# Decoder layer on eight cores: three filler matmul units per attention step in place of four, and the normalizer's small DMAs issued by SyncE in place of GpSimd

## The chip, the cores and the metric

The kernel runs on one Trainium2 chip, on all 8 of its cores. Each core computes half of the query rows of one of four sequences; the cores do not talk to each other. The metric is the device time in microseconds of the slowest core.

## The reference

One transformer layer with the normalization behind each residual, in float32, x of shape (4, 4096, 1024), 16 heads of 64, hidden size 3072:

```python
def reference(x, Wq, Wk, Wv, Wo, w_gate, w_up, w_down):
    x = _layernorm(x + attn(x, Wq, Wk, Wv, Wo))   # causal softmax attention, scale 1/8
    x = _layernorm(x + ffn(x, w_gate, w_up, w_down))
    return x

def ffn(x, w_gate, w_up, w_down):                 # int weights, times 1/127
    h = silu(x @ wg.T) * (x @ wu.T)
    return h @ wd.T
```

## The kernel before

All activations are kept feature-major (features on partitions, tokens along the free axis). A core holds the whole sequence's keys and values (T = 4096) and 2048 of its queries, taken as every second block of 128 tokens, so that the causal work is even. The text cuts the program into three parts: attention (to about 1283 us), the output projection with the first normalization, and the feed-forward part with the second. The change touches the first part alone.

Attention runs in NPASS = 4 passes, numbered 0 to 3, of four heads each. A pass `p` needs keys, values and queries of its heads. Pass 0's are projected ahead of everything (`proj_gen(0)`, run to its end); those of pass `p + 1` are projected during pass `p`, as filler between the attention matmuls. Between two passes stands `c_compute` (lines 278 to 325), a serial chain that finds the bound by which the exponent is shifted.

`attention_pass` (lines 388 to 490) loops over 2 head pairs (`hp`) and 4 banks of 512 queries (`bank`); bank number b sees 8b + 8 key blocks (`kb`), so the banks have 8, 16, 24 and 32 steps and a pass has 2 x 80 = 160 steps. One step:

- `emit_s` of the next key block: two score matmuls into `sp` (lines 398 and 403, one head each, on the two halves of TensorE's rows), then one exponential over both heads on ScalarE (line 415), 128 x 1024 elements. `sp` and `pt` have two buffers each. In the last 8 steps of a bank the block lies on the causal diagonal: the tile narrows to 384, 256 and 128 queries, and VectorE multiplies two masks (lines 421 and 424).
- `fill(rate)`: takes `rate` units from the filler generator (line 471).
- `emit_pv` of the current block: two matmuls of the probabilities with the values into `op` (line 443).

At a bank's end VectorE copies both heads' outputs and row sums out of PSUM (lines 477 and 483, four copies), and the first `emit_pv` of the next bank waits for the last of them. SyncE stores the row sums in DRAM (`ldram`, line 486).

The filler. `proj_gen(p + 1)` has 448 units, one matmul each. For each of 8 slices of 512 tokens there are 16 key units of 512 columns (line 226) and then 32 value units of 256 columns (line 240); after these come 4 query slices of 16 units of 512 columns (line 264). The text calls the 192 key and query units wide and the 256 value units narrow. Eight units make a group that VectorE then copies out of PSUM (`pp`, two buffers). The slices of x come through GpSimd's DMA queue with a cast to bf16 into `xstg`, two buffers: each load waits until the slice before the last is used up (lines 219 and 257). The weights of a pass come at the generator's start on the same queue (lines 194 to 196), with no wait of their own.

Behind the 448 units the filler chain has `norm_gen(p - 1)`, 10 more units, in passes 1, 2 and 3 (in pass 3 it is the only filler); for the last pass it runs by itself at the end (line 508). It turns the row sums of pass `p - 1` into reciprocals and scales the outputs. When it is called, ahead of the pass, its first part (lines 330 to 334) is emitted: the queue waits for the row sums' stores and loads them into `lrecA`. Its first unit is a reciprocal on VectorE, and a store `linvd<-lrecB` that waits for it; its second is eight loads `lpair<-linvd` that wait for that store (`s_lwb`); each of the other eight is one float32 matmul that spreads `lpair` over the partitions (line 366, shown as two instructions) and a multiplication on VectorE (line 371). Before the change all of these DMAs stand on GpSimd's queue, between the loads of x and the weights. Each queue issues in program order, and an instruction that waits holds everything behind it.

The semaphores that matter: `s_ldm` (row sum stores landed), `s_lpr` (`lrecA` landed), `s_nrm` (reciprocal done), `s_lwb` (`linvd` landed), `s_lp` (`lpair` landed), `s_xst` (x landed), `s_evV` (VectorE copies).

Of the kernel before, what the change touches and what calls it, by code (L numbers as in the profile page):

```python
# [42 lines left out]
def build_program(cfg):  # L43
# [16 lines left out]
    nc = bass.Bass("TRN2", target_bir_lowering=False, num_devices=1)  # L60
# [22 lines left out]
    with st:  # L83
# [15 lines left out]
        s_evV = Sem(st, nc, "s_evV")  # L99
# [5 lines left out]
        s_ldm = [Sem(st, nc, f"s_ldm{i}") for i in range(4)]  # L105
        s_lpr = Sem(st, nc, "s_lpr")
        s_lwb = Sem(st, nc, "s_lwb")
        s_lp = [Sem(st, nc, f"s_lp{i}") for i in range(8)]
        s_cb = Sem(st, nc, "s_cb")
        s_nrm = Sem(st, nc, "s_nrm")  # L110
# [217 lines left out]

        def norm_gen(p):
            for i in range(4):  # L330
                nc.gpsimd.wait_ge(s_ldm[i].h, s_ldm[i].n)
            s_lpr.inc(nc.gpsimd.dma_start(
                lrecA[:, :], ldram[4 * p:4 * p + 4].rearrange("h (a f) -> (h a) f", f=LRF)), 16)
            lrd = s_lpr.n

            def gen():
                nc.vector.wait_ge(s_lpr.h, lrd)
                s_nrm.inc(nc.vector.reciprocal(lrecB[:, :], lrecA[:, :]))
                nc.gpsimd.wait_ge(s_nrm.h, s_nrm.n)
                s_lwb.inc(nc.gpsimd.dma_start(  # L340
                    linvd[4 * p:4 * p + 4].rearrange("h (a f) -> (h a) f", f=LRF),
                    lrecB[:, :]), 16)
                wb = s_lwb.n
                yield
                idxs = [(2 * p + g, s) for g in range(2) for s in range(NQS)]
                ldone = {}
                def issue(i):
                    gcx, s = idxs[i]
                    j = lp_slot[0]
                    lp_slot[0] = (j + 1) % 8  # L350
                    nc.gpsimd.wait_ge(s_lwb.h, wb)
                    nc.gpsimd.wait_ge(s_evV.h, ldone.get(("f", j), 0))
                    s_lp[j].inc(nc.gpsimd.dma_start(
                        lpair[j][:, :],
                        linvd[2 * gcx:2 * gcx + 2, s * 512:s * 512 + 512]), 16)
                    ldone[i] = (j, s_lp[j].n)
                for i in range(len(idxs)):
                    issue(i)
                yield
                for i, (gcx, s) in enumerate(idxs):  # L360
                    j, lv = ldone[i]
                    pi = gidx[0] % 2
                    gidx[0] += 1
                    nc.tensor.wait_ge(s_evV.h, pp_free[pi])
                    nc.tensor.wait_ge(s_lp[j].h, lv)
                    s_prj.inc(nc.tensor.matmul(pp[pi][:, :], emat[:, :], lpair[j][:, :],
                                               start=True, stop=True))
                    tgt = s_prj.n
                    nc.vector.wait_ge(s_prj.h, tgt)
                    q0 = s * 512  # L370
                    s_evV.inc(nc.vector.tensor_mul(
                        ofm[:, gcx * TOWN + q0: gcx * TOWN + q0 + 512],
                        ofm[:, gcx * TOWN + q0: gcx * TOWN + q0 + 512], pp[pi][:, :]))
                    pp_free[pi] = s_evV.n
                    ldone[("f", j)] = s_evV.n
                    yield
            return gen()

        def chaing(*gens):
            for g in gens:  # L380
                yield from g
# [113 lines left out]
        for p in range(NPASS):  # L495
            parts = []
            if p + 1 < NPASS:
                parts.append(proj_gen(p + 1))
            if p >= 1:
                parts.append(norm_gen(p - 1))  # L500
            filler = chaing(*parts) if parts else None
            filler = attention_pass(p, filler, rate=4)
            if filler is not None:
                for _ in filler:
                    pass
            if p + 1 < NPASS:
                c_compute(p + 1)
        for _ in norm_gen(NPASS - 1):
            pass
# [184 lines left out]
        for idx, (ncx, s) in enumerate(wo_iters):  # L694
            q0 = s * 512
            i = idx % 2
            j = idx % 4
# [101 lines left out]
        for fs in range(NFS):  # L799
# [79 lines left out]
            for dc in range(NCH):  # L879
# [11 lines left out]
                for nh in range(NH2):  # L891
                    c0 = nh * 512
                    i = 0
# [110 lines left out]
```

## Time and profile before

| what | us |
|---|---|
| median of 2 runs | 2122.15 (2077.97 and 2166.32) |
| profiled execution | 2078.7 |
| its span on the slowest core (core 4) | 2077.7 |
| spans of the eight cores | 2051.9 to 2077.7 |
| TensorE busy | 1618.6 (78%) |
| ScalarE busy | 824.3 (40%) |
| VectorE busy | 613.9 (30%) |
| GpSimd busy | 183.8 (9%) |
| mean granted TensorE clock of the cores | 0.861 to 0.873 |

Busy times are unions over the whole span, which has stages with different limits, so their shares say nothing of a single stage. The rows of the trace all come from core 4. The clock column of a view is the clock that TensorE was granted, as a share of its full speed: 1.00 is the upper of its two levels (2.4 GHz), 0.50 the lower (1.2 GHz), and what lies between is a mean over a stretch that had both.

### The profile page before, as it was taken

Reading aid. Unit: us, or ns where it says so; the run is one execution under the profiler, and the core shown is the slowest. Engines: PE = TensorE matmul, PEld = TensorE weight load, DVE = VectorE, ACT = ScalarE, POOL = GpSimd, SP = SyncE. Lnnn points to the kernel's source line nnn. Section 1 sums busy time; section 2 is a strip of 40 time slices with the busy share of each in tenths; the row PEclk is TensorE's granted clock in tenths of the full one; section 3 lists DMA queues with packets and bytes.
Section 4 is the critical chain, followed back from the end, with each engine's and each line's share of the span. In section 5 each row is a group of like instructions: output and inputs, shape, how many; then the busy total and the mean of one; then the engine's idle time right before and its main releaser. Section 6 shows DMA issues by size and latency. Waiting matters only on the chain. (4 is left out here: it accounts for less than half of the span.)

```text
span 2077.7 us, 22780 instructions; the slowest of 8 cores (2051.9 to 2077.7 us)
## 1 busy us (share of the span) xinstructions
PE 1618.6 (78%) x7240; PEld 625.2 (30%) x7240; DVE 613.9 (30%) x1436; ACT 824.3 (40%) x999; POOL 183.8 (9%) x221
## 2 busy tenths in 40 slices
PE   3858998679977689887577674877998879998862
PEld 1423443124432134321111111323443334443320
DVE  1234332253332432421521212454211111111224
ACT  0015665756654767537367670331111011112022
POOL 1010000010000000010100001001221112221000
PEclk9887999879997799978578785988999999999985
DMA  7692333063340433320000003325777657777522
GB/s 100 94 136 36 62 62 61 1 93 62 51 72 2 57 56 62 61 43 1 3 1 1 1 1 58 91 65 52 69 74 71 61 51 71 71 72 71 86 56 81
DMA packets 224112, 115.31 MB, mean 55 GB/s; under 512 B 152030, under 2 KB 215520, under 8 KB 224000
## 3 DMA queue, kind: packets, MB, share of 16 engines
q0 software_dynamic: 215104, 96.94, 38.1%
q1 hardware_dynamic: 8896, 16.91, 2.6%
q8 instruction: 65, 1.06, 0.2%
q14 instruction: 47, 0.39, 0.1%
HBM read 201.66 MB, written 8.65 MB: 101 GB/s over the span
## 5 line engine op out<-in xcount | busy, mean ns | idle before, releaser
L415 ACT ACTIVATE pt<-sp,cbias 128x1024 bf16<-128x1024 f32 (+3 forms) x640 | 619.7, 984 | 384.2 <-PE sp L403 380.3
L443 PE MATMUL op<-pt,vbuf 128*65 128x512 bf16 (+3 forms) x1280 | 376.4, 379 | 144.5 <-DVE pt L424 57.4
L398 PE MATMUL sp<-qbuf,kbuf 64*128 64x512 bf16 (+3 forms) x640 | 239.2, 383 | 2.1 <-DVE cbias L324 2.1
L403 PE MATMUL sp<-qbuf,kbuf 64*128 64x512 bf16 (+3 forms) x640 | 239.5, 383 | 0.0
L443 PEld LDWEIGHTS op<-pt,vbuf 128*65 128x65 bf16 x1280 | 118.8, 117 | 291.2 <-issue 259.8
L899 PE MATMUL dps<-hbuf,wdd 128*128 128x512 bf16 x768 | 179.8, 393 | 34.1 <-DVE y L910 32.9
L841 PE MATMUL gps<-x1b,wgb 128*128 128x512 bf16 x768 | 186.9, 387 | 24.0 <-DVE x1b L809 13.0
L850 PE MATMUL ups<-x1b,wub 128*128 128x512 bf16 x768 | 184.7, 384 | 6.8 <-DVE hbuf L862 6.8
L858 ACT ACTIVATE sgb<-gps 128x512 bf16<-128x512 f32 x96 | 57.3, 597 | 304.5 <-PE gps L841 295.1
L226 PE MATMUL pp<-xstg,wkb 128*128 128x512 bf16 x512 | 142.7, 414 | 40.4 <-DMA xstg<-xfm 40.4
L240 PE MATMUL pp<-wvb,xstg 128*128 128x256 bf16 x1024 | 150.1, 278 | 0.6
L862 DVE TENSOR_TENSOR hbuf<-sgb,ups 128x512 bf16<-128x512 bf16 x96 | 66.1, 688 | 285.2 <-PE ups L850 285.2
L421 DVE TENSOR_TENSOR pt<-pt,mka 128x128 bf16<-128x128 bf16 x128 | 28.8, 225 | 366.9 <-ACT pt L415 366.7
L398 PEld LDWEIGHTS sp<-qbuf,kbuf 64*128 64x128 bf16 x640 | 58.1, 94 | 250.4 <-issue 248.5
L574 ACT ACTIVATE ysq<-y 128x512 bf16<-128x512 f32 x64 | 40.0, 625 | 219.7 <-DVE y L910 134.8
L899 PEld LDWEIGHTS dps<-hbuf,wdd 128*128 128x128 bf16 x768 | 75.0, 100 | 140.9 <-issue 62.8
L841 PEld LDWEIGHTS gps<-x1b,wgb 128*128 128x128 bf16 x768 | 74.4, 99 | 124.3 <-issue 42.8
L850 PEld LDWEIGHTS ups<-x1b,wub 128*128 128x128 bf16 x768 | 76.0, 99 | 100.7 <-issue 12.8
L297 ACT ACTIVATE qsq<-kbuf 128x512 bf16<-128x512 bf16 x64 | 39.4, 627 | 165.1 <-DVE qbuf L272 142.6
L240 PEld LDWEIGHTS pp<-wvb,xstg 128*128 128x128 bf16 x1024 | 85.0, 99 | 48.8 <-issue 34.9
L264 PE MATMUL pp<-xstg,wqb 128*128 128x512 bf16 x256 | 72.6, 421 | 27.6 <-DMA xstg<-xq 27.4
L252 DVE CAST vbuf<-pp 128x256 bf16<-128x256 f32 x128 | 54.4, 425 | 120.0 <-PE pp L240 118.6
(83 smaller groups left out, 1218.2 us busy)
## 6 DMA issues: line engine op xcount, KB each, us to landing
xstg<-xfm POOLq DMA_DIRECT2D x32, 1024.0 KB, 9.4
xstg<-xq POOLq DMA_DIRECT2D x16, 1024.0 KB, 9.3
wgb<-wgT POOLq DMA_DIRECT2D x48, 256.0 KB, 4.3
wub<-wuT POOLq DMA_DIRECT2D x48, 256.0 KB, 5.4
wdd<-wdT POOLq DMA_DIRECT2D x16, 768.0 KB, 8.1
xres<-xq SPq DMA_DIRECT2D x32, 256.0 KB, 3.3
yout<-y SPq DMA_DIRECT2D x4, 2048.0 KB, 6.9
wqb<-wqT POOLq DMA_DIRECT2D x4, 512.0 KB, 8.0
```

The lines of the kernel that those rows point to most:

```text
L226: return nc.tensor.matmul(ps[:, 0:512], wkb[pb][:, m * PD + nk * 128: m * PD + nk * 128 + 128], xs[:, m * 512:(m + 1) * 512], start=(m == ...
L240: return nc.tensor.matmul(ps[:, 0:PD], xs[:, m * 512 + jb * 128: m * 512 + jb * 128 + 128], wvb[pb][:, m * PD:(m + 1) * PD], start=(m == 0 ...
L264: return nc.tensor.matmul(ps[:, 0:512], wqb[pb][:, m * PD + nq * 128: m * PD + nq * 128 + 128], xs[:, m * 512:(m + 1) * 512], start=(m == ...
L398: nc.tensor.matmul(sp[buf][:, js * 128: 512], kbuf[pb][0:64, hp * T + kb * 128: hp * T + kb * 128 + 128], qbuf[pb][0:64, hp * TOWN + qbase ...
L403: s_s.inc(nc.tensor.matmul(sp[buf][:, 512 + js * 128: 1024], kbuf[pb][64:128, hp * T + kb * 128: hp * T + kb * 128 + 128], qbuf[pb][64:128 ...
L415: s_exp.inc(nc.scalar.activation(pview, sview, AF.Exp, bias=cbias[pb][:, 0:1]))
L443: lastpv = nc.tensor.matmul(ops[hl][:, js * 128: 512], vbuf[pb][:, kb * VGW + (2 * hp + hl) * 65: kb * VGW + (2 * hp + hl) * 65 + 65], pt[ ...
L841: lastg = nc.tensor.matmul(gps[:, :], wgb[wi][:, m * 128:(m + 1) * 128], x1b[:, m * FFS + c0: m * FFS + c0 + 512], start=(m == 0), stop=(m ...
L850: last = nc.tensor.matmul(ups[:, :], wub[wi][:, m * 128:(m + 1) * 128], x1b[:, m * FFS + c0: m * FFS + c0 + 512], start=(m == 0), stop=(m ...
L858: s_fact.inc(nc.scalar.activation(sgb[:, :], gps[:, :], AF.Silu))
L862: s_fdve.inc(nc.vector.tensor_mul(hbuf[:, hc * FFS + c0: hc * FFS + c0 + 512], sgb[:, :], ups[:, :]))
L899: last = nc.tensor.matmul(dps[i][:, :], wdd[wi2][:, hc * 128: hc * 128 + 128], hbuf[:, hc * FFS + c0: hc * FFS + c0 + 512], start=(hc == 0 ...
```

## The change

Two edits in the attention part. `norm_gen` issues its DMAs, and makes its waits, on SyncE's queue instead of GpSimd's. `attention_pass` is called with `rate=3` instead of `rate=4`: `fill` takes three units per step.

```diff
         def norm_gen(p):
             for i in range(4):
-                nc.gpsimd.wait_ge(s_ldm[i].h, s_ldm[i].n)
-            s_lpr.inc(nc.gpsimd.dma_start(
+                nc.sync.wait_ge(s_ldm[i].h, s_ldm[i].n)
+            s_lpr.inc(nc.sync.dma_start(
                 lrecA[:, :], ldram[4 * p:4 * p + 4].rearrange("h (a f) -> (h a) f", f=LRF)), 16)
             lrd = s_lpr.n
 
             def gen():
                 nc.vector.wait_ge(s_lpr.h, lrd)
                 s_nrm.inc(nc.vector.reciprocal(lrecB[:, :], lrecA[:, :]))
-                nc.gpsimd.wait_ge(s_nrm.h, s_nrm.n)
-                s_lwb.inc(nc.gpsimd.dma_start(
+                nc.sync.wait_ge(s_nrm.h, s_nrm.n)
+                s_lwb.inc(nc.sync.dma_start(
                     linvd[4 * p:4 * p + 4].rearrange("h (a f) -> (h a) f", f=LRF),
                     lrecB[:, :]), 16)
@@
-                    nc.gpsimd.wait_ge(s_lwb.h, wb)
-                    nc.gpsimd.wait_ge(s_evV.h, ldone.get(("f", j), 0))
-                    s_lp[j].inc(nc.gpsimd.dma_start(
+                    nc.sync.wait_ge(s_lwb.h, wb)
+                    nc.sync.wait_ge(s_evV.h, ldone.get(("f", j), 0))
+                    s_lp[j].inc(nc.sync.dma_start(
                         lpair[j][:, :],
                         linvd[2 * gcx:2 * gcx + 2, s * 512:s * 512 + 512]), 16)
@@
-            filler = attention_pass(p, filler, rate=4)
+            filler = attention_pass(p, filler, rate=3)
```

TensorE, in pass 1, where the filler runs out: the last query units and the first matmuls of the normalizer (`pp<-lpair,emat`), and the first step that has no filler. Before:

```order
L264 MATMUL pp1<-xstg1,wqb0 128x512 x4
L443 MATMUL op0<-pt1,vbuf1 65x512
L443 MATMUL op1<-pt1,vbuf1 65x512
L398 MATMUL sp1<-qbuf1,kbuf1 128x512
L403 MATMUL sp1<-qbuf1,kbuf1 128x512
L366 MATMUL pp0<-lpair0,emat 128x512
L366 MATMUL pp1<-lpair1,emat 128x512
L443 MATMUL op0<-pt0,vbuf1 65x512
L443 MATMUL op1<-pt0,vbuf1 65x512
```

And now, the same place in the filler:

```order
L264 MATMUL pp1<-xstg1,wqb0 128x512 x3
L443 MATMUL op0<-pt0,vbuf1 65x512
L443 MATMUL op1<-pt0,vbuf1 65x512
L398 MATMUL sp0<-qbuf1,kbuf1 128x512
L403 MATMUL sp0<-qbuf1,kbuf1 128x512
L264 MATMUL pp1<-xstg1,wqb0 128x512
L443 MATMUL op0<-pt1,vbuf1 65x512
L443 MATMUL op1<-pt1,vbuf1 65x512
L398 MATMUL sp1<-qbuf1,kbuf1 128x512
L403 MATMUL sp1<-qbuf1,kbuf1 128x512
L366 MATMUL pp0<-lpair0,emat 128x512
```

The number of matmuls is the same. Before, 448 units at 4 a step end with step 112 of the pass, inside the last bank but one; now, at 3 a step, with the first unit of step 150, ten steps before the end. In both, one pair of `op` matmuls and one pair of `sp` matmuls stand between the last projection unit and the first matmul that reads `lpair`.

GpSimd's queue from the last x load of pass 0 on (`xstg<-xq` are the query slices), as a difference:

```order
 L186 DMA xstg<-xfm 128x8x512 x8
 L186 DMA xstg<-xq 128x8x512 x4
-L332 DMA lrecA<-ldram 32x256
 L191 DMA wqb<-wqT 128x8x256
 L191 DMA wkb<-wkT 128x8x256
```

With `lrecA` gone from this queue, nothing stands between the last x load of one pass and the weights of the next: they and the next two x slices are no longer held until the row sums of the pass are stored.

SyncE's queue in passes 0 and 1 (after it, the same for the others):

```order
-L486 DMA ldram<-lstg 1x512 x64
+L486 DMA ldram<-lstg 1x512 x16
+L332 DMA lrecA<-ldram 32x256
+L486 DMA ldram<-lstg 1x512 x14
+L340 DMA linvd<-lrecB 32x256
+L353 DMA lpair<-linvd 2x512 x8
+L486 DMA ldram<-lstg 1x512 x2
```

The normalizer's DMAs now stand between the row sum stores of the seventh and of the last bank of the pass.

## Rows read from the trace of the kernel before

**Rows 1.** Windows, passes 0 to 3: us; busy PE, PEld, DVE, ACT, POOL; PEclk, DMA share, GB/s.
```profile
170.40:411.50 241.10, 207.33 (x1088) 81.60 (x1088) 70.59 (x212) 156.07 (x162) 8.73 (x10) 0.93 0.28 45
438.30:704.80 266.50, 225.45 (x1106) 87.07 (x1106) 80.45 (x227) 158.43 (x164) 13.47 (x19) 0.89 0.27 42
728.90:991.40 262.50, 223.26 (x1106) 86.19 (x1106) 80.29 (x227) 157.53 (x164) 13.45 (x19) 0.90 0.27 43
1015.50:1258.00 242.50, 170.27 (x656) 45.20 (x656) 52.03 (x170) 152.95 (x160) 4.68 (x9) 0.76 0.00 1
```

**Rows 2.** Timeline, pass 0: start, us, engine, line; a wide-filled step, then a narrow-filled one.
```profile
250.78 0.39 PE L398 MATMUL sp<-qbuf,kbuf 64*128 64x512 bf16 x1
...
251.10 1.04 PE L226 MATMUL pp<-xstg,wkb 128*128 128x512 bf16 x4
...
251.97 0.59 PE L443 MATMUL op<-pt,vbuf 128*65 128x512 bf16 x2
...
252.50 0.39 PE L398 MATMUL sp<-qbuf,kbuf 64*128 64x512 bf16 x1
...
253.80 0.39 PE L398 MATMUL sp<-qbuf,kbuf 64*128 64x512 bf16 x1
```

**Rows 3.** Timeline, pass 0: steps without filler, two exponentials a row.
```profile
380.76 2.13 ACT L415 ACTIVATE pt<-sp,cbias 128x1024 bf16<-128x1024 f32 x2 [0.20 <-PE sp L403]
...
383.09 2.13 ACT L415 ACTIVATE pt<-sp,cbias 128x1024 bf16<-128x1024 f32 x2 [0.20 <-PE sp L403]
```

**Rows 4.** Windows: pass 0's filled banks 2 and 3, query units, empty bank; pass 3's banks 2, 3.
```profile
208.80:243.90 35.10, 33.29 (x196) 14.49 (x192) 11.49 (x33) 24.05 (x24) 1.79 (x3) 1.00 0.39 61
243.90:290.60 46.70, 44.97 (x260) 19.82 (x256) 13.70 (x37) 32.95 (x32) 2.56 (x3) 1.00 0.44 69
303.20:335.30 32.10, 26.28 (x132) 10.80 (x128) 9.80 (x29) 15.14 (x16) 1.75 (x2) 0.84 0.52 82
371.10:411.50 40.40, 29.60 (x128) 7.69 (x124) 5.49 (x20) 32.81 (x34) 0.00 (x0) 0.88 0.00 1
1071.80:1104.00 32.20, 23.36 (x98) 5.99 (x96) 5.66 (x21) 23.38 (x24) 0.00 (x0) 0.82 0.00 1
1104.00:1145.60 41.60, 31.33 (x130) 8.03 (x128) 5.62 (x21) 31.97 (x32) 0.00 (x0) 0.83 0.00 1
```

**Rows 5.** Timeline, TensorE: a change of bank at full clock; a filled step at half clock.
```profile
246.81 0.59 PE L443 MATMUL op<-pt,vbuf 128*65 128x512 bf16 x2 [1.58 <-DVE lstg L483]
...
438.94 0.63 PE L398 MATMUL sp<-qbuf,kbuf 64*128 64x512 bf16 x1
...
442.20 0.50 PE L398 MATMUL sp<-qbuf,kbuf 64*128 64x384 bf16 x1
```

**Rows 6.** Who waited for whom in pass 1 (438 to 704): total us, times, longest.
```profile
PE pp L366 <- DMA lpair<-linvd: 6.6, 1, 6.6
...
PE pp L264 <- DMA xstg<-xq: 3.0, 1, 3.0
```

**Rows 7.** The normalizer in pass 1: its timeline, and the window that holds it.
```profile
622.50 0.54 POOL L340 DMA_DIRECT2D linvd<-lrecB  x1 [18.96 <-DVE lrecB L338]
624.88 4.30 POOL L353 DMA_DIRECT2D lpair<-linvd  x8 [1.85 <-DMA linvd<-lrecB]
626.78 3.75 PE L366 MATMUL pp<-lpair,emat 2*128 2x512 f32 x4 [6.57 <-DMA lpair<-linvd]
...
618.10:647.40 29.30, 22.73 (x43) 6.59 (x42) 7.84 (x10) 5.57 (x5) 4.73 (x9) 0.59 0.01 2
```

**Rows 8.** DMA issues of the whole run: median us to landing.
```profile
xstg<-xq POOLq DMA_DIRECT2D x16, 1024.0 KB, 9.3
```

**Rows 9.** Tile `lrecA`, all four passes; its loads' time to landing.
```profile
DMA to landing us min/median/max: 1.9/2.6/3.4
```

**Rows 10.** Timeline, the end of attention: last row sum stores, first load of the normalizer.
```profile
1255.73 1.64 SPq L486 DMA_DIRECT2D ldram<-lstg  x2
...
1258.78 0.53 POOL L332 DMA_DIRECT2D lrecA<-ldram  x1 [230.38 <-DMA ldram<-lstg]
```

## The prediction

> **What bounds the kernel now.** I read the windows of the four passes first. Passes 0, 1 and 2 take 241.1, 266.5 and 262.5 us, pass 3, which has no projection in it, 242.5 [rows 1]: 448 filler matmuls cost a pass next to nothing, so a filled pass must have slack in its empty part. The timeline shows where. A full-width step with four wide units takes 1.72 us, from 250.78 to 252.50, and TensorE never stops: scores 0.32, filler 0.87, `op` pair 0.53. With four narrow units it takes 1.30, to 253.80 [rows 2]. Two steps without filler take 2.33 us, one 1.165, and there the exponential sets the pace, two in 2.13 us and 0.20 of waiting [rows 3]; TensorE's own work is 0.32 + 0.53 = 0.85, so it idles 0.31 in each. Before the change a pass has 112 filled steps and 48 empty ones: TensorE-bound first, ScalarE-bound after.
>
> The clock adds to it. The filled banks 2 and 3 ran at a granted clock of 1.00, the bank with the query units at 0.84, the empty bank at 0.88, and pass 3's at 0.82 and 0.83 [rows 4]. The falls to half clock come after TensorE waited or had little to do. At half clock a wide-filled step takes 3.26 us, 438.94 to 442.20 [rows 5].
>
> **The rate.** The same 448 units now need 149 1/3 steps, and 10 2/3 stay empty. A wide unit takes 0.87 / 4 = 0.22 us, a narrow one half, 0.11. A step with three wide units then takes 1.72 - 0.22 = 1.50, with three narrow ones 1.19, still just above 1.165. At full clock and with every step of full width:
> - before: 48 wide steps x 1.72 + 64 narrow x 1.30 + 48 empty x 1.165 = 221.7 us
> - after: 64 x 1.50 + 85.3 x 1.19 + 10.7 x 1.165 = 209.9 us, 11.8 less.
>
> Not all of this arrives. At a change of bank TensorE idles 1.58 us behind VectorE's fourth copy though it has four wide units there [rows 5]; six changes, three steps each, lose a unit and gain nothing: 18 x 0.15 = 2.7 back. In the narrow masked steps the chain exponential, mask, `op` is about as long as the filled step; some 14 of them give back about 2.7. That leaves 6.4. The same step-by-step sum makes the filled banks of before 35.0 and 47.0 us; measured are 35.1 and 46.7 [rows 4]. For after it gives them 31.9 and 42.7, and pass 3's empty ones, which are a floor, took 32.2 and 41.6 with the clock at 0.82: the filler becomes nearly free.
>
> Two smaller terms per pass. A slice of query units was used up in 4 x 1.72 = 6.9 us while its successor takes 9.3 to land [rows 8], and TensorE waited 3.0 us in pass 1 [rows 6]. A slice now lasts 5 1/3 x 1.50 = 8.0; two slices cover 2.2 us more, I take 2.0. And the clock: the step sum at full clock gives pass 0 of before 227 us; measured are 241.1, of which some 4 is the waiting for x and 10 the half clock, most of it in the query bank and the empty steps. Those steps now have filler and shorter waits; I take 4 of the 10 back, the fall at the start of a pass stays. Bounds: 0 and 8.
>
> So 6.4 + 2.0 + 4 = 12.4 us per pass, three passes, -37. What is late next in each step is again TensorE, but with ScalarE 0.03 us behind it in the narrow ones. Pass 3 has only the ten normalizer units; three instead of four a step moves one matmul by a step: 0.
>
> **The normalizer on SyncE.** In the timeline its chain is 622.50 (store), 624.88 (first load), 626.78 (first matmul); TensorE waits 6.57 us at it, and the stretch around it runs at a clock of 0.59 [rows 6, 7]. At rate 3 the same two pairs of matmuls stand between the last query unit and the first `lpair` matmul, so the wait stays. What is queued behind the waiting instructions on SyncE is only row sum stores: in passes 1 and 2 those of the last bank, issued after the normalizer is through, and four `lstg` buffers stand before VectorE would wait for one. Cost 0. GpSimd's issue took 2.38 us from store to load; SyncE's last row sum store, whose issue ended at 1255.73 + 1.64 = 1257.37, had landed by 1258.78 [rows 10], 1.4 later, for a smaller transfer. I take the hop as equal, bounds -1 and +1 us for each of four chains: 0, between -4 and +4.
>
> The Trainium skill, "DMA: Bandwidth & Descriptors", section "Latency and other measured facts", puts the first byte at about 0.6 us for a DMA issued from SyncE and about 1 us from GpSimd. By it three hops in four chains would save 3 x 4 x 0.4 = 4.8 us and the sum would be five lower; no row here times the same transfer on both queues.
>
> The new thing is what GpSimd now does early. With `lrecA` off its queue, the three weight loads for the next projection follow the last x load at once and two x slices follow as their buffers come free, in passes 0 and 1. Their old place was under `c_compute`, where the filler did not wait for them, so issuing them earlier gains 0. But in pass 1 they are in flight when the normalizer's store and loads run. The row for a small load beside such traffic: `lrecA` took up to 3.4 us to land, 1.9 at the least [rows 9], 1.5 more. Two transfers in the chain, once: +3; bounds 0 and +10, if each waits out half of a 9.3 us slice. The last x load of passes 0 and 1 shares with the weights too and its successor has none to wait for; under 1 us each, within the rounding.
>
> Sum: -37 + 3 = -34. The profiled execution took 2078.7 us around a span of 2077.7, close to the lower of the two runs shown (2077.97); the median 2122.15 is only the mean of it with 2166.32. My forecast stands against 2078.7: 2078.7 - 34 = about 2045 us, 1.6% less. Two per cent is about what a measurement of this kernel can tell from no change.
>
> **Rivals.**
> - Only the step sum arrives: the half clock keeps its 10 us a pass and the wait for x its 3. 3 x 6.4 = 19, less 3 for the normalizer: 2063 us. For it: the falls also come at masked steps, which stay light. Against: the filled banks 2 and 3 had none [rows 4].
> - More arrives: the clock stays up in the whole filled stretch, 8 us a pass, and the wait for x goes: 3 x 17 = 51, 2028 us. The floor is pass 3: 242.5 less the 20 us of its own normalizer leaves 222, so three passes cannot give more than about 58, 2020 us.
> - The normalizer is caught behind the early loads: +10 in place of +3, 2052 us.
> - Slower: thinner filler lets the clock fall at every change of bank. Four narrow units a step kept it at 1.00 there, none did not (pass 3, 0.82 and 0.83) [rows 4], and three lie between. Where it falls with filler present TensorE is the bound: a narrow step goes from 1.19 to about 2.4 us, and over a fall of three such steps that is 3.5 us. Seven changes in three passes are 21 x 3.5 = 74 us: 2045 + 74 = 2119 us. It decides from about ten falls on, 34 / 3.5; below that the change still gains. Against it: three narrow units still leave TensorE busy all through an ordinary step (1.19 of 1.19), and a full-width step with no filler at all held full clock in pass 0.
> - The edits change nothing that counts, since filler moves only from where TensorE is the bound to where it has slack, and ScalarE takes the gain back by waiting more often at the masked steps: 2078 us. Against it: 15 us of idle TensorE in 48 steps are real.
>
> On the slower rival, the Trainium skill, "TensorE: Matmul & The Clock Gate", section "Part 1: The HAM clock gate (the "warmup" mystery)", says that "the default state is throttled, and activity releases the throttle". The rows on the clock above agree in direction: 0.88 and 0.82 where TensorE is thinly loaded, 1.00 where it is full. By the rule alone thinner filler speaks for more falls in the filled part and fewer in what was empty.
>
> **How the numbers follow.** Forecast, 2035 to 2055: 0.52. Step sum only, near 2063: 0.17. More arrives, near 2028: 0.15. Normalizer caught: 0.06. Nothing: 0.05. Slower by the clock: 0.05. The unknown costs (clock 0 to 8 a pass, hops -4 to +4, collision 0 to +10) carry the forecast to 2022 and 2070, and that range leaves out mainly the last two cases. Faster by over 2% means under 2037: the "more" case and the lower edge of the forecast, 0.20. Slower by over 2%, over 2120, is the upper part of the clock rival: 0.04. Within 2%: 0.76.
>
> **What would show it.** In the profile of the changed kernel: wide steps of 1.50 and narrow ones of 1.19 us; full banks 2 and 3 near 32 and 43 us; query units ending inside the last bank of a pass; the three filled passes near 229, 257 and 251 us and pass 3 unchanged; TensorE's wait for `xstg<-xq` under 2 us a pass; its wait for `lpair` at 6 to 7 us in pass 2 and longer in pass 1; weight loads issued before the pass ends. I am wrong if the clock in banks 1 to 3 falls well below 1.00, if narrow steps stay at 1.30, or if the wait at `lpair` grows past 15 us.

## The result, and the profile after

The changed kernel took 2068.68 us (median of 21 executions) where the kernel before took 2088.11 (median of 18). The ratio is 0.9906, with a 95% interval from 0.9874 to 0.9937: about 20 us less, a real gain, but one inside the 2 per cent and well short of the 34 us forecast. The profiled execution took 2055.78 us around a span of 2054.7, 22.9 under that of before. That agrees with the ratio, and it is the number the forecast of 2045 stands against: 11 us too fast. In some executions one half of the chip ran at a lower clock and took some per cent longer; the medians are over all executions, the ratios leave those out.

First the windows of passes 0 to 3 on core 4, the columns as in [rows 1]:

```profile
164.90:404.00 239.10, 211.66 (x1090) 80.26 (x1090) 71.26 (x214) 158.31 (x164) 13.15 (x15) 0.92 0.41 60
429.60:694.00 264.40, 226.76 (x1106) 84.43 (x1106) 80.38 (x227) 159.00 (x164) 13.15 (x15) 0.87 0.37 55
717.90:974.00 256.10, 227.02 (x1106) 84.67 (x1105) 80.01 (x227) 158.97 (x164) 8.76 (x10) 0.89 0.27 42
998.20:1238.00 239.80, 168.23 (x656) 44.55 (x654) 51.96 (x169) 153.26 (x160) 0.00 (x0) 0.77 0.00 1
```

Against [rows 1] the passes are 2.0, 2.1, 6.4 and 2.7 us shorter; 12 had been forecast for each filled one. The clock column is what to look at: 0.93, 0.89, 0.90 before, 0.92, 0.87, 0.89 now. It did not rise, it fell. The early loads show in GpSimd's column of pass 0, 15 issues for 10 and 13.15 us for 8.73. In pass 1 it has 15 for 19, though the normalizer's nine are gone. The DMA share rose with them, from 0.28 to 0.41 and from 0.27 to 0.37.

One core is a thin basis for a few microseconds, so from here on I also use means over the eight cores of a profile, from the first score matmul of a pass to the start of its last, read in each core's timeline. "Half clock" is 2 x (1 - granted clock) x length, the time spent at the lower level. The last column ends with the issue of the first load of the output projection's weights.

| mean of 8 cores, us | pass 0 | pass 1 | pass 2 | pass 3 | last score to output projection |
|---|---|---|---|---|---|
| before | 238.5 | 260.9 | 259.9 | 234.7 | 30.7 |
| after | 232.6 | 258.9 | 250.1 | 233.8 | 28.3 |
| half clock before | 28.7 | 54.2 | 53.6 | 101.0 | |
| half clock after | 27.8 | 59.3 | 49.2 | 101.2 | |

Together 5.9 + 2.0 + 9.8 + 0.9 + 2.4 = 21 us, which is the ratio's 20. Pass 1 gained next to nothing, and the half clock kept its total.

The steps themselves are as the sum had them. TensorE's timeline on core 4, a step with three wide units (242.72 to 244.22) and one with three narrow ones (246.71 to 247.89):

```profile
242.72 0.39 PE L398 MATMUL sp<-qbuf,kbuf 64*128 64x512 bf16 x1
...
243.04 0.82 PE L226 MATMUL pp<-xstg,wkb 128*128 128x512 bf16 x3
...
244.22 0.39 PE L398 MATMUL sp<-qbuf,kbuf 64*128 64x512 bf16 x1
...
246.71 0.39 PE L398 MATMUL sp<-qbuf,kbuf 64*128 64x512 bf16 x1
...
247.03 0.50 PE L240 MATMUL pp<-wvb,xstg 128*128 128x256 bf16 x3
...
247.89 0.39 PE L398 MATMUL sp<-qbuf,kbuf 64*128 64x512 bf16 x1
```

Now the banks. The windows of pass 0's filled banks 2 and 3, of the fifth bank (the first of the second half) and of its last one, against [rows 4]:

```profile
200.90:234.70 33.80, 30.52 (x170) 12.23 (x168) 9.59 (x30) 23.96 (x24) 1.09 (x2) 0.95 0.20 33
234.70:277.80 43.10, 40.38 (x228) 15.91 (x226) 11.52 (x33) 32.99 (x32) 1.82 (x3) 1.00 0.31 50
277.80:292.60 14.80, 12.27 (x59) 4.49 (x56) 7.10 (x24) 6.25 (x8) 0.59 (x1) 0.77 0.46 72
348.00:401.00 53.00, 43.92 (x188) 14.03 (x184) 10.78 (x26) 32.43 (x31) 6.76 (x8) 0.89 0.93 129
```

Bank 3 took 43.10 at full clock; 42.7 was the step sum. Bank 2 took 33.80 at 0.95 where 31.9 was the sum. The fifth bank ran at 0.77. TensorE's timeline at its start shows how that comes about (a score pair that reads `qbuf,kbuf` opens each step):

```profile
277.77 0.38 PE L398 MATMUL sp<-qbuf,kbuf 64*128 64x512 bf16 x1
...
278.08 0.82 PE L226 MATMUL pp<-xstg,wkb 128*128 128x512 bf16 x3
281.10 1.04 PE L443 MATMUL op<-pt,vbuf 128*65 128x512 bf16 x2 [2.20 <-DVE pt L424]
282.07 0.50 PE L398 MATMUL sp<-qbuf,kbuf 64*128 64x384 bf16 x1
...
284.75 0.50 PE L398 MATMUL sp<-qbuf,kbuf 64*128 64x384 bf16 x1
...
287.22 0.28 PE L398 MATMUL sp<-qbuf,kbuf 64*128 64x256 bf16 x1
```

Three wide units end, TensorE idles 2.20 us behind VectorE's mask, and the `op` pair after it takes 1.04 in place of 0.59: the lower level. The next two steps, masked ones of 384 queries, take 2.68 and 2.47 us (from 282.07 and from 284.75); the one behind them takes 1.29. By 287 the clock is back.

Last the wait for the normalizer in pass 1. These are the waits of TensorE there on core 4; in [rows 6] they were 6.6 and 3.0 (as means of the eight cores `lpair` takes 12.2 now and 6.6 before):

```profile
PE pp L366 <- DMA lpair<-linvd: 9.6, 1, 9.6
PE pp L264 <- DMA xstg<-xq: 4.8, 1, 4.8
```

And the timeline around it, against [rows 7]:

```profile
630.30 0.88 POOL L186 DMA_DIRECT2D xstg<-xq  x1 [7.23 <-PE pp L264]
631.17 0.88 POOL L191 DMA_DIRECT2D wqb<-wqT  x1
...
645.19 0.88 POOL L186 DMA_DIRECT2D xstg<-xfm  x1 [11.38 <-PE pp L264]
653.46 0.88 POOL L186 DMA_DIRECT2D xstg<-xfm  x1 [7.38 <-PE pp L264]
655.44 0.31 SPq L340 DMA_DIRECT2D linvd<-lrecB  x1
661.87 2.84 SPq L353 DMA_DIRECT2D lpair<-linvd  x8
663.29 5.45 PE L366 MATMUL pp<-lpair,emat 2*128 2x512 f32 x6 [9.64 <-DMA lpair<-linvd]
```

The weight load goes out right behind the last `xstg<-xq` and two slices of the next projection follow, the second 2 us before the 32 KB store `linvd`. The store takes 655.44 to 661.87. The view of tile `linvd` gives its four landings:

```profile
DMA to landing us min/median/max: 1.4/1.4/6.3
```

Three take 1.4 us, the one beside the megabyte takes 6.3. The DMA issues of the run show the same of the larger loads: `xstg<-xq` has a median of 9.7 (9.3 in [rows 8]), and the weights, which now share with the last x load:

```profile
wqb<-wqT POOLq DMA_DIRECT2D x4, 512.0 KB, 13.4
```

### The profile page after: what moved, and what is told of

It reads as the page before. It is cut to its first block and busy times, and to the rows that moved or that the text cites. A ratio compares the mean times of both kernels' runs of the same rounds, so it can differ in the third digit from the quotient of the medians.

```text
span 2054.7 us, 22780 instructions; the slowest of 8 cores (2028.8 to 2054.7 us)
## 1 busy us (share of the span) xinstructions
PE 1621.6 (79%) x7240; PEld 617.6 (30%) x7240; DVE 612.3 (30%) x1436; ACT 828.1 (40%) x999; POOL 163.0 (8%) x181
## 5 line engine op out<-in xcount | busy, mean ns | idle before, releaser
L226 PE MATMUL pp<-xstg,wkb 128*128 128x512 bf16 x512 | 148.9, 409 | 40.3 <-DMA xstg<-xfm 39.6
L240 PE MATMUL pp<-wvb,xstg 128*128 128x256 bf16 x1024 | 164.0, 281 | 0.6
L421 DVE TENSOR_TENSOR pt<-pt,mka 128x128 bf16<-128x128 bf16 x128 | 28.8, 225 | 249.0 <-ACT pt L415 247.6
## 6 DMA issues: line engine op xcount, KB each, us to landing
wqb<-wqT POOLq DMA_DIRECT2D x4, 512.0 KB, 13.4
```

The costliest lines, as they stand in the source:

```text
L226: return nc.tensor.matmul(ps[:, 0:512], wkb[pb][:, m * PD + nk * 128: m * PD + nk * 128 + 128], xs[:, m * 512:(m + 1) * 512], start=(m == ...
L240: return nc.tensor.matmul(ps[:, 0:PD], xs[:, m * 512 + jb * 128: m * 512 + jb * 128 + 128], wvb[pb][:, m * PD:(m + 1) * PD], start=(m == 0 ...
```

## The experiments

All times are medians of 5 to 13 executions, each beside runs of the kernel before on the same chip; the interval of each ratio is the 95% one.

**The rate alone.** The kernel before, `norm_gen` left on GpSimd:

```diff
-            filler = attention_pass(p, filler, rate=4)
+            filler = attention_pass(p, filler, rate=3)
```

> The rate alone: three units a step, the normalizer's DMAs left on GpSimd's queue, so that the next pass's loads stay behind the row sums. Theory C (collision): the changed kernel lost time in passes 0 and 1 because the weights and x slices of the next projection, now issued early, slow the last x load and the normalizer's two small transfers. Then passes 0 and 1 are about 4 and 8 us shorter here than in the changed kernel (from first to last score matmul near 229 and 251 us, where the changed kernel has 232.6 and 258.9 as a mean over cores and before has 238.5 and 260.9), and the whole is about 10 us faster than the changed kernel: ratio to before 0.985. Theory K (clock): the gain was lost to falls of TensorE's clock at bank changes under thinner filler. Then passes 0 and 1 are as in the changed kernel and the ratio is 0.991 to 0.993 (the normalizer's hops on GpSimd cost 3 us more).

Measured: 0.9871 [0.9837, 0.9904], 2056.57 us. Filled passes 231.4, 253.3, 253.2: 7.1, 7.6 and 6.7 shorter than before. That is the step sum's 6.4 with 0.3 to 1.2 more. TensorE's wait for x falls from 4.0, 3.2 and 3.4 us to 2.4, 2.5 and 2.3 (means of the eight cores), 1.1 of the 2.0 on average. Of the 4 for the clock nothing came: the half clock is 27.2, 54.0 and 53.1 us.

**The queue alone.** The changed kernel with four units a step:

```diff
-            filler = attention_pass(p, filler, rate=3)
+            filler = attention_pass(p, filler, rate=4)
```

> The queue alone: the normalizer on SyncE, four units a step. Theory C: passes 0 and 1 get slower than before by the same collisions (3 to 10 us together), the four normalizer chains win about 1 us each; ratio 0.998 to 1.004, TensorE's wait for lpair in pass 1 over 10 us. Theory K: no collision of weight, ratio 0.998, wait for lpair in pass 1 near 5 us.

Measured: 1.0000 [0.9974, 1.0025]. Pass 1 takes 268.4, 7.5 longer than before; passes 0 and 2 are within 1.0. The wait for `lpair` in pass 1 is 10.8 on its slowest core. What the queue gives at the end of each chain (below) is paid back in pass 1.

**The early loads held back.** The changed kernel, with GpSimd waiting for the row sums again before it issues a new projection's loads, and all else on SyncE:

```diff
             parts = []
+            if p >= 1:
+                for i in range(4):
+                    nc.gpsimd.wait_ge(s_ldm[i].h, s_ldm[i].n)
```

> The changed kernel with one wait put back on GpSimd's queue: the loads of the next projection wait for the row sums of the pass, as before the change. Theory C: the best of all: pass 0 near 229, pass 1 near 250 us, pass 2 unchanged at 250; ratio 0.983 to 0.985. Theory K: as the changed kernel, 0.99.

Measured: 0.9848 [0.9820, 0.9876], 2054.90 us. Pass 1 takes 251.3, 7.6 less than with the change; pass 0 takes 230.6, 2.0 less; pass 2, where no early load was, 249.6 against 250.1. All four landings of `linvd` are short again, in the view of the tile:

```profile
DMA to landing us min/median/max: 1.4/1.4/1.5
```

and so is TensorE's wait in pass 1, by the list of waits:

```profile
PE pp L366 <- DMA lpair<-linvd: 4.8, 1, 4.8
```

**The same at four units a step**, which closes the square of rate and loads:

```diff
-            filler = attention_pass(p, filler, rate=3)
+            filler = attention_pass(p, filler, rate=4)
```

> The missing corner: normalizer on SyncE, loads held, four units a step. If the collision is all that cost the queue change its gain, pass 1 falls from 268.4 (queue alone) to about 259 us, the four chains keep their 2 us each, and the ratio is 0.995 to 0.998, where the queue alone gave 1.000. If instead the order of the loads does not matter at four units a step, 1.000 and 268 us.

Measured: 0.9955 [0.9921, 0.9988]. Pass 1 is 259.9 and not 268.4. Beside the kernel before, passes 1, 2 and 3 are 1.0, 2.1 and 2.3 us shorter and the end 2.4, 7.8 in all: that is SyncE's part. So the early loads cost 0.45% at rate 4 (to 1.0000) and 0.58% at rate 3 (0.9848 to 0.9906), 9 and 12 us of 2088. SyncE by itself gives 0.45% at rate 4 (from 1) and 0.23% at rate 3 (from 0.9871), 9 and 5 us. Each of these differences is about as large as the intervals it is made of, but passes and waits agree with all four.

**Three x buffers**, in the changed kernel, the loads early as there:

```diff
-        slot_free = [0, 0]
+        slot_free = [0, 0, 0]
...
-                slot = ts % 2
+                slot = ts % 3
...
-                slot = qs % 2
+                slot = (NKVS + qs) % 3
```

> The changed kernel with three buffers for the x slices, so that the last query slices are loaded a slice earlier. Both theories: TensorE's wait for xstg<-xq in passes 0 to 2 (3 to 4 us each) goes, and with it one fall of the clock each. If a wait costs only itself, 10 us less than the changed kernel (0.986); if the half clock after it costs as much again, up to 15. Theory C adds that the wait for lpair in pass 1 stays long (over 10 us), since the next projection's loads still run beside it.

Measured: 0.9704 [0.9675, 0.9732], 2026.64 us. The filled passes give 4.6, 2.5 and 2.3. The large part is ahead of them: pass 0 starts at 139.3 on the mean and not at 160.2. TensorE's waits in this stretch, first with the change (0 to 165), then here (0 to 140):

```profile
PE pp L226 <- DMA xstg<-xfm: 39.6, 5, 28.9
PE pp L264 <- DMA xstg<-xq: 16.0, 3, 8.4
```

```profile
PE pp L226 <- DMA xstg<-xfm: 28.5, 1, 28.5
PE pp L264 <- DMA xstg<-xq: 7.5, 2, 5.3
```

The first wait, for the first slice, stays; the others go or halve. The profile's stretches account for some 30 of the 42 us between the ratios 0.9906 and 0.9704; the profiled executions are 33.7 apart, and each ratio has an interval of about 6 us to either side. I did not place the rest. In pass 1 the last bank still holds the collision (pass 1 is 256.4, pass 2 247.8): TensorE waits 15.8 us for `lpair` there on the slowest core.

**Three buffers and the loads held**:

```diff
+            if p >= 1:
+                for i in range(4):
+                    nc.gpsimd.wait_ge(s_ldm[i].h, s_ldm[i].n)
```

> Held loads and three x buffers together. If collision and the wait for x add up: passes 0, 1, 2 near 226, 249, 247 us, the start of pass 0 some 22 us earlier than before the change (the x loads of the first projection), ratio 0.965. If three buffers make the collision harmless (loads early enough), no better than three buffers alone, 0.970.

Measured: 0.9699 [0.9673, 0.9725]. Pass 1 gives the 10 us (246.0), the ratio hardly any (0.9704 before): pass 2 is 1.6 longer and the rest is within the interval. With three buffers the ratio alone would not show the collision; the passes do.

**More filler at a change of bank.** The loads held, and six units in the first step of each bank:

```diff
-                        fill(rate)
+                        fill(6 if kb == 0 else rate)
```

> The version with the held loads, but six units instead of three in the first step of each bank, where TensorE otherwise idles behind VectorE's fourth copy. Theory K2: what ate the rest of the forecast are falls of TensorE's clock at the changes of bank, which four units a step did not have in the full banks (0 us at half clock in banks 2 and 3 of a pass before, 2 to 3 us each at three units). Then these falls become fewer, pass 0 goes from 230.6 to 226 to 228 us as a mean over cores, and the ratio from 0.985 to 0.980 to 0.982. Rival (units only): where a unit stands makes no difference; the filler only ends some eight steps earlier, pass 0 stays within 1 us of 230.6 and the ratio at 0.985.

Measured: 0.9769 [0.9734, 0.9805], 2039.79 us, 0.8% under the run with the loads held alone. Half clock of pass 0 falls from 25.6 to 13.3 us and the pass from 230.6 to 224.3. The windows of bank 3 and of the fifth bank, of this kernel (its slowest core, 2) and then of the run with the loads held (core 4):

```profile
239.20:281.60 42.40, 40.30 (x227) 16.22 (x227) 11.80 (x34) 32.96 (x32) 1.75 (x2) 1.00 0.37 57
281.60:293.00 11.40, 9.20 (x63) 3.98 (x59) 6.88 (x24) 6.24 (x8) 0.00 (x0) 1.00 0.35 58
```

```profile
238.40:283.00 44.60, 41.88 (x226) 16.19 (x226) 11.46 (x33) 32.99 (x32) 1.77 (x3) 0.96 0.30 48
283.00:297.80 14.80, 12.27 (x58) 4.46 (x56) 7.09 (x24) 6.24 (x8) 0.65 (x1) 0.77 0.46 72
```

The fifth bank goes from 14.80 at 0.77 to 11.40 at 1.00. The timeline of its first step shows the same wait, only shorter, and no fall: the `op` pair behind it has its 0.59:

```profile
281.96 1.04 PE L226 MATMUL pp<-xstg,wkb 128*128 128x512 bf16 x4
282.83 0.38 PE L240 MATMUL pp<-wvb,xstg 128*128 128x256 bf16 x2
284.95 0.59 PE L443 MATMUL op<-pt,vbuf 128*65 128x512 bf16 x2 [1.73 <-DVE pt L424]
```

This edit also moves units between steps, so in the sum of the pass the filler and the clock are mixed. The fifth bank of the changed kernel itself settles it: the same instructions were run there at three clocks. In order, core 1 in pass 2, core 1 in pass 1, core 4 in pass 2:

```profile
825.90:837.90 12.00, 9.52 (x60) 3.98 (x56) 7.11 (x24) 6.25 (x8) 0.66 (x1) 1.00 0.58 89
541.10:554.50 13.40, 10.92 (x58) 4.15 (x56) 7.01 (x24) 6.25 (x8) 0.63 (x1) 0.87 0.51 80
830.90:845.50 14.60, 12.11 (x58) 4.43 (x56) 6.97 (x24) 6.25 (x8) 0.58 (x1) 0.77 0.46 73
```

2 x (1 - 0.77) x 14.60 = 6.7 us of half clock cost 2.6 us of time, 0.4 for each.

The traces bear a count as well. Take as a fall any change of bank with over 1 us at the lower level in the 9 us behind the bank's first score matmul; there are 7 changes x 3 passes x 8 cores = 168. The kernel before has 77 falls, the changed one 119, the one with the loads held 111, and this one 60. Bank 2 is where this edit does not reach: it starts with narrow units, six of them are only 0.66 us of filler, and it falls in 22 of 24. But the sixth bank starts with six narrow ones too and has no fall, so the filler of the first step is not all that counts.

**The normalizer's store and loads early.** The loads held, and the normalizer's first two units (the reciprocal with its store, and the eight loads) put ahead of the projection:

```diff
+            ng = norm_gen(p - 1) if p >= 1 else None
+            if p >= 1:
+                parts.append(head(ng))
             if p + 1 < NPASS:
                 parts.append(proj_gen(p + 1))
             if p >= 1:
-                parts.append(norm_gen(p - 1))
+                parts.append(ng)
```

> The version with the held loads, with the normalizer's reciprocal and its nine small DMAs at the head of the filler instead of behind the 448 projection units; its matmuls stay at the end. If TensorE's wait for lpair is what starts the half-clock stretch at the normalizer (5 to 6 us of waiting, 30 us at half clock in the last bank of passes 1 and 2), both go: passes 1 and 2 shorter by 8 to 15 us each, ratio near 0.975. Rival: the normalizer's two-row float32 matmuls keep the clock down by themselves; then only the wait goes, 5 us a pass, ratio near 0.980, and the half clock stays above 20 us.

Measured: 0.9838 [0.9807, 0.9868] beside 0.9848: no difference in the ratio. Pass 1 takes 247.6 against 251.3 and pass 2 247.9 against 249.6. The wait is gone from the last bank of pass 1, which goes from 69.5 to 62.7 (the other banks give 3 us of that back), but 23.0 us of half clock stay in it (29.7 before). So the wait causes only the smaller part of the low clock around the normalizer.

**All of it, and the filler metered by columns.** Three buffers, loads held, normalizer early; each unit now yields its cost (wide 2, narrow 1, normalizer 2), and a step takes units until it has spent 4, or 10 at the start of a bank:

```diff
-                for _ in range(n):
-                    if next(filler, StopIteration) is StopIteration:
+                credit[0] += n
+                while credit[0] > 0:
+                    cost = next(filler, StopIteration)
+                    if cost is StopIteration:
...
+                    credit[0] -= cost or 2
...
-                        fill(rate)
+                        fill(10 if kb == 0 else rate)
```

> All of it, and the filler metered by columns: two wide or four narrow units a step (the same TensorE time), five or ten in a bank's first step. By the step rows a full step then takes 1.29 whatever its filler, in place of 1.51 and 1.19. Theory K2: with the load even and the change of bank filled, the clock falls less in the full banks and pass 0 ends near 218 to 223 us; ratio 0.945 to 0.955. Units only: about as three a step, pass 0 near 226, ratio near 0.957.

Measured: 0.9424 [0.9400, 0.9448], 1962.67 us, with the next one the fastest of all and 2.75% under three buffers with the loads held (0.9699). That is the gain of three edits together, the early normalizer, the filler at the change of bank and the metering; they were not taken apart at this point. A filled step gets about two wide or four narrow units, 0.44 us, where the change gives 0.66 in some and 0.33 in others. The last ten steps or so of a pass have no projection unit in either. None of the 168 changes of bank has a fall; TensorE's waits there are 1.27 to 1.74 us, where the changed kernel has 1.79 to 2.20 and 119 falls. Passes 0 and 1, pass 0's bank 3 and its fifth bank, and the last bank of pass 1, on the slowest core (6):

```profile
139.90:353.00 213.10, 197.46 (x1084) 77.47 (x1080) 69.51 (x209) 156.02 (x159) 7.86 (x9) 0.99 0.30 45
382.20:607.60 225.40, 211.69 (x1098) 81.25 (x1094) 76.88 (x219) 156.12 (x159) 7.87 (x9) 0.95 0.33 51
205.00:247.40 42.40, 40.79 (x229) 16.59 (x227) 11.54 (x34) 32.96 (x32) 1.75 (x2) 1.00 0.39 58
247.40:258.80 11.40, 9.51 (x68) 4.74 (x66) 7.09 (x25) 6.24 (x8) 0.00 (x0) 1.00 0.35 57
555.90:607.60 51.70, 48.64 (x183) 15.19 (x179) 14.81 (x33) 32.48 (x31) 0.11 (x1) 0.87 0.13 21
```

Pass 0 has 4.6 us of half clock left of 27.8, and takes 213.3 us. In passes 1 and 2 it is 24, and nearly all of that (19.8 in pass 1) in the last bank, where the normalizer stands. TensorE's timeline there shows where the level falls: the same four instructions go from 1.98 to 3.78 us after the second group, with no wait named ahead of them (13.7 us stay at the lower level on this core from 590.4 on):

```profile
585.53 1.98 PE L366 MATMUL pp<-lpair,emat 2*128 2x512 f32 x4
588.32 1.98 PE L366 MATMUL pp<-lpair,emat 2*128 2x512 f32 x4
591.60 3.78 PE L366 MATMUL pp<-lpair,emat 2*128 2x512 f32 x4
596.84 3.78 PE L366 MATMUL pp<-lpair,emat 2*128 2x512 f32 x4
```

**The normalizer's matmuls spread.** As above, with one normalizer unit behind each 48th projection unit and at a cost of 8:

```diff
+        def mixed(pg, ng):
+            for i, cost in enumerate(pg):
+                if ng is not None and i < 384 and i % 48 == 47:
+                    yield next(ng)
+                yield cost
```

> The column-metered version with one normalizer matmul behind every 48th projection unit instead of all eight behind the last. In the version before it the last bank of passes 1 and 2 took 53.6 us against pass 0's 40.1, with 20 us at half clock. If the normalizer's float32 matmuls are slow because they stand together at half clock (1.8 us each), alone among projections at full clock they take about half and passes 1 and 2 come to 218 to 221 us from 227; ratio 0.934 to 0.938. Rival: each costs the same wherever it stands, or pulls the clock down around it: 224 to 230 us, ratio 0.942 or above.

Measured: 0.9427 [0.9383, 0.9471], no change. But the profile differs: the half clock of pass 1 goes from 24.3 to 7.9 us and the pass from 226.5 to 221.1 (pass 2 from 227.0 to 221.8), while the stretches behind the two passes grow from 29.2 to 32.2 and 31.8. The edit itself does that: at a cost of 8 the filler costs 640 + 64 + 4 = 708 and a pass spends 160 x 4 + 8 x 6 = 688, so ten query units are left over and run behind passes 1 and 2. Spread singly, the two-row matmuls no longer bring the level down, but they are not free: the other seven banks of pass 1 are 6.9 us longer together, the last one 12.3 shorter. What is left of the gain, 2.4 and 2.6 us behind passes 1 and 2, is less than the ratio can tell.

## Why the prediction was wrong

**The step sum was right.** Wide steps of 1.51 and narrow ones of 1.19 us stand in the timeline (1.50 and 1.19 forecast); bank 3 took 43.1 for 42.7. The rate alone gave 7.1, 7.6 and 6.7 us a pass, for 6.4 by the steps and 12.4 in all.

**The step that failed is "I take 4 of the 10 back" with the wait's 2.0 beside it**, 6.0 of the 12.4 us a pass. The clock did come up where the prediction had it: in pass 0, the sixth bank, which had held the query units and the wait for x, went from 8.1 us of half clock to 1.3, and the last one, empty before, from 9.1 to 5.6. It fell elsewhere in exchange: bank 2 from 0 to 3.4, bank 3 from 0 to 1.3 and the fifth bank from 0 to 5.5 (means of the eight cores). In total 28.7 became 27.8.

And it moved to where it costs. In an empty step ScalarE is the bound, so a slow TensorE is mostly hidden: a full-width one takes 1.53 us at the lower level for 1.165, one with three narrow units 2.15 for 1.19. Bank by bank, over all cores and runs, each us of half clock goes with 0.40 to 0.47 us of time in the second to seventh of the eight banks of the filled passes (three units a step) and with 0.15 to 0.21 in the third to eighth of pass 3 (the slope over all cores of the runs). At 0.45 and 0.2, an estimate, the half clock of pass 0 cost about 10 us before, as the prediction had it, and about 12 after: not 4 back but 2 more.

The prediction held this as its slower rival, with 21 falls at 3.5 us. The mechanism was real; its size was not. A core has on average 15 falls at its 21 changes, but it had 10 before; each costs 1.5 us (3.4 us of half clock) to 2.6, and they offset a gain and no more. The experiment with more filler in the first step of each bank shows it by its other side: half the half clock gone, 6.3 us of pass 0, of which 12.3 x 0.4 is about 5. The argument "three narrow units still leave TensorE busy all through an ordinary step" looked at the ordinary step; the level is lost in the one that is not, at the change of bank, where the wait behind VectorE is longer the less filler stands before it (2.20 us behind three wide units, 1.73 behind six units).

The floor of 222 us that the prediction took from pass 3, by which three passes could give no more than 58 us, was none: pass 3 runs with 101 us of half clock. The version metered by columns has pass 0 at 213.3, and its three filled passes are 92 us shorter than before.

As for the wait for x, as means of the eight cores: 4.0, 3.2 and 3.4 us before; 3.2, 2.9 and 1.5 now; 2.2, 2.4 and 2.0 with the loads held. So the longer slice covers 1.1 to 1.3 of the 2.0 a pass, and in passes 0 and 1 the early loads take half or more of that away.

**The collision was right in kind and too small**: "+3" was taken for one transfer pair in pass 1, and the last x loads of passes 0 and 1 were put "within the rounding". By the loads held back the two together cost 7.6 us in pass 1 and 2.0 in pass 0, 9 to 12 us by the ratios. I priced the store by what `lrecA` took beside other traffic, 1.5 us more [rows 9]; `linvd` took 6.3 for 1.4, 4.9 more, and the wait it makes then adds low clock (37.9 us of half clock in the last bank of pass 1 against 29.7 with the loads held). In size the collision is the rival "caught behind the early loads", +10, which had been given 0.06.

**The hop to SyncE was not 0** but a gain: TensorE's wait for `lpair` falls from 6.6 to 4.8 us where nothing else is in flight, and the stretch from the last score matmul to the output projection from 30.7 to 28.3. `linvd` lands in 1.4 us from SyncE and in 1.7 from GpSimd, and its issue takes 0.31 for 0.53. The Trainium skill, "DMA: Bandwidth & Descriptors", section "Latency and other measured facts", has 0.6 and 1 us for the two paths; I set its 4.8 us aside for want of a row. The runs are nearer to it: 2.4 us for the last chain, 5 to 9 for all four by the ratios. Its other line there, that access to memory goes from 0.2 us on average to 2 under high load, agrees in sign with the late store, which was 4.9 us later, more than that line speaks of.

Put together by the ratios: rate -27 (forecast -37), SyncE -5 (0), early loads +12 (+3), in all -20 (-34). By the passes the rate gives 21; the 27 is known to 7 us. The signs of the rate and of the early loads held, that of the clock did not. 2078.7 - 20 = 2059: the rival "only the step sum arrives", 2063 us, was the nearest, and it had been given 0.17. It was near partly by luck, since the gain on SyncE, which it leaves out, and the larger collision nearly cancel.

Pass 3 was forecast unchanged and is (233.8 against 234.7).

## What to carry to other kernels

Where filler keeps TensorE at its upper clock, count it at the weakest step, not at the average one: thinning it everywhere to fill the empty steps moved the lower level into the part where TensorE is the bound. Meter filler by the time it takes and not by the number of units, and give more where a wait is known to come; with the normalizer's early start that was worth three times the change. When a wait is taken off a queue, list the bulk loads that it had held back and what small dependent transfers they will now run beside.

## What the runs showed of the hardware

- A run of two-row float32 matmuls kept TensorE busy and did not keep its clock up. In the last bank of pass 1 of the kernel metered by columns 19.8 us (mean of the cores) were at the lower level, with no wait for `lpair` and with the loads held; the level fell behind the second group of four. Spread singly among bf16 projections they left 7.9 us of half clock in the whole pass. The Trainium skill, "TensorE: Matmul & The Clock Gate", section "Part 1: The HAM clock gate (the "warmup" mystery)", speaks of activity that releases the throttle; here the level fell while no wait of TensorE stands in the rows. Whether two rows, float32 or something else about these steps does it was not measured.
- A us at the lower level cost about 0.4 us where TensorE was the bound and about 0.2 where ScalarE was.
- With 1.1 us of filler in a bank's first step (five wide or ten narrow units) the level fell at none of 168 changes of bank; with three units, at 119.
- The same instructions in the same bank took 12.00, 13.40 and 14.60 us at 1.00, 0.87 and 0.77 of the clock.
- A 32 KB store beside megabyte loads landed in 6.3 us, alone in 1.4. 512 KB of weights landed in 13.4 us beside the last x load (median of four), and in 8.0 and 7.9 where they were held.
- A third x buffer, thought of for the passes, took 21 us off the stretch ahead of them.
